# An S4 and quantized-FFN layer on one core: the first x parts paired, and gate/up block 0 cut into a chunk of its own

## The reference

```
x = x + 0.5 * ffn(layernorm(x));  x = x + s4(layernorm(x));  x = x + 0.5 * ffn(layernorm(x))

def _qlinear(x, q, scale, A, Bm):
    w = (q.astype(jnp.float32) - Q_ZERO) * (scale * Q_STEP)[:, None]
    y = jnp.einsum('bsh,oh->bso', x, w)
    return y + LR_SCALE * (x @ A @ Bm)

ffn(x) = _qlinear(silu(_qlinear(x, gate...)) * _qlinear(x, up...), down...)
s4(u)  = irfft(rfft(u, n=2L) * rfft(K, n=2L))[..., :L] + D * u      # K from the S4 state, L = 512
```

## Time and profile before

| what | value |
|---|---|
| median of three executions | 569.65 us (569.47 to 571.22) |
| the profiled execution | 569.99 us, span 568.2 us |
| PE busy | 556.5 us, 98% of the span |
| DVE, ACT, POOL busy | 427.2, 312.9, 256.4 us |
| PE clock granted over the span | full speed in every one of the 40 slices |
| bytes read from HBM, written | 15.90 MB, 4.19 MB |
| PE busy in 0 to 20 us, 20 to 64 us, 64 to 100 us | 20.00, 43.22, 35.26 us (pipelined matmuls overlap) |

### The profile page before, as it was taken

The page is one execution under the profiler, slowest core; times in us unless marked ns, Lnnn a source line. Parts: engine busy times, 40 slices in busy tenths (PEclk is TensorE's granted clock), DMA queues, the critical chain, the costliest instruction groups (busy, mean ns, idle before and its releaser), DMA issues.

```text
span 568.2 us, 12661 instructions
## 1 busy us (share of the span) xinstructions
PE 556.5 (98%) x4816; PEld 449.4 (79%) x4816; DVE 427.2 (75%) x824; ACT 312.9 (55%) x773; POOL 256.4 (45%) x272
## 2 busy tenths in 40 slices
PE   8999999989999999999999999999999999999997
PEld 8644678887688877888778887788877888788975
DVE  5789889996889957889578884598845987555544
ACT  5778425863168831688317883178731676246621
POOL 4379612664036850368503784037830477015510
PEclk9999999999999999999999999999999999999999
DMA  8985431009050190002900029000391104440002
GB/s 262 340 282 204 86 59 43 2 1 131 15 22 5 30 180 15 2 2 35 175 16 2 1 38 171 15 3 1 59 151 55 37 2 56 84 158 2 2 0 75
DMA packets 90804, 40.04 MB, mean 70 GB/s; under 512 B 79000, under 2 KB 84889, under 8 KB 90745
## 3 DMA queue, kind: packets, MB, share of 16 engines
q1 hardware_dynamic: 89849, 38.97, 31.3%
q10 hardware_dynamic: 896, 0.27, 0.2%
HBM read 15.90 MB, written 4.19 MB: 35 GB/s over the span
## 4 chain that ended last, share of the span: by engine, by line
PE 92%; DVE 5%; issue 1%; ACT 1%; DVEq 1%; POOL 0%; POOLq 0%; ACTq 0%
PE banks L1561 40%; PE banks L1480 28%; PE banks L1523 6%; PE banks L1537 5%; PE banks L1706 5%; PE banks L1432 2%; PE banks L1716 2%; PE banks L1500 1%; PE banks L1517 1%; PE banks L1726 1%; DVE X L1050 0%; DVE c_stats L1080 0%; DVE ring L1047 0%; DVEq L909 0%; PE banks L1415 0%
## 5 line engine op out<-in xcount | busy, mean ns | idle before, releaser
L1561 PE MATMUL banks<-xT,w 128*128 128x256 f16 (+1 forms) x2156 | 260.4, 273 | 1.5 <-DVE work L1006 1.4
L1561 PEld LDWEIGHTS banks<-xT,w 128*128 128x128 f16 (+1 forms) x2156 | 212.5, 100 | 26.3 <-DVE work L1006 2.7
L1480 PE MATMUL banks<-dw,hT 128*128 128x256 f16 (+3 forms) x1408 | 184.0, 286 | 0.0
L1480 PEld LDWEIGHTS banks<-dw,hT 128*128 128x128 f16 (+1 forms) x1408 | 135.4, 98 | 33.8 <-issue 0.4
L1006 DVE SCALAR_TENSOR_TENSOR work<-banks,work 128x512 f32<-128x512 f32 (+1 forms) x88 | 60.6, 688 | 43.4 <-PE banks L1523 27.4
L501 POOL TENSOR_TENSOR rstd<-veps,minus_half 128x1 f32<-128x1 f32 x32 | 19.6, 615 | 160.8 <-DVE veps L912 160.7
L571 POOL TENSOR_SCALAR hT<-work 128x512 f16<-128x512 f32 x70 | 44.2, 631 | 99.6 <-DVE work L1006 99.6
L574 POOL TENSOR_TENSOR hT<-work,hT 128x512 f16<-128x512 f32 x70 | 82.6, 1179 | 5.8
L1020 DVE SCALAR_TENSOR_TENSOR banks<-banks,scales,work 128x512 f32<-128x512 f32 (+1 forms) x77 | 57.7, 750 | 0.7 <-PE banks L1561 0.7
L1027 DVE SCALAR_TENSOR_TENSOR banks<-banks,scales,work 128x512 f32<-128x512 f32 (+1 forms) x77 | 57.7, 750 | 0.2 <-ACT work L807 0.2
L581 POOL TENSOR_TENSOR z<-zs,z 128x1024 f16<-128x1024 f32 (+1 forms) x28 | 55.5, 1992 | 4.5 <-ACT z L740 4.4
(11 more groups left out here) (191 smaller groups left out, 677.2 us busy)
## 6 DMA issues: line engine op xcount, KB each, us to landing
out_x<-X SPq DMA_DIRECT2D x15, 256.0 KB, 2.8
X<-in_x SPq DMA_DIRECT2D x1, 2048.0 KB, 9.9
ring<-in_gate_q_t SPq DMA_DIRECT2D x2, 768.0 KB, 9.5
hT<-in_up_q_t SPq DMA_DIRECT2D x2, 768.0 KB, 11.3
X<-in_b SPq DMA_DIRECT2D x2, 560.0 KB, 10.7
X<-in_x SPq DMA_DIRECT2D x1, 1024.0 KB, 14.3
ring<-in_down_q_t SPq DMA_DIRECT2D x1, 1024.0 KB, 12.5
X<-in_x SPq DMA_DIRECT2D x3, 256.0 KB, 5.0
```

The source lines that it names most:

```text
L1480: last = mm(acc(j)[:, 1 - c, 0:width], hT[0:rows[m], m, a, j * P:(j + 1) * P], dw[0:rows[m], m, src], start=(m == 0 and a == 0), stop=(m = ...
L1561: last = mm(dst[0:r, 0:HH], w[:, blocks + k, cols], xT[:, a, 2 * op + k, :], start=(first and k == 0 and a == 0), stop=(k == 1 and a == 1) ...
```

## The change

Three things are edited. The first two parts of x come in as one pair of transfers: SP loads both parts of partitions 0 to 63, ACT both parts of partitions 64 to 127, and DVE's statistics of part 0 and of part 1 both wait for the two transfers. `CHUNKS` becomes five groups: block 0 alone, then 1 to 3, 4 and 5, 6 and 7, and 8 to 10; the transfers of chunks 2 and 3 stand where chunk 2's stood. POOL casts chunk 0 ahead of the fourth rstd instead of behind it, chunk 3 right behind chunk 2, and chunk 4 where chunk 3 was cast; ACT casts chunks 2, 3 and 4 at m = 2, 4 and 6.

```diff
-CHUNKS = [(0, 2), (2, 5), (5, 8), (8, 11)]
+CHUNKS = [(0, 1), (1, 4), (4, 6), (6, 8), (8, 11)]
...
-            sp.dma_start(X[0:P // 2, 0, :], x_v[0:P // 2, 0, :]).then_inc(s_x[0], 16)
-            for j in range(1, TS):
+            sp.dma_start(X[0:P // 2, 0:2, :], x_v[0:P // 2, 0:2, :]).then_inc(s_x[0], 16)
+            for j in range(2, TS):
                 sp.dma_start(X[:, j, :], x_v[:, j, :]).then_inc(s_x[j], 16)
...
             chunk(2)
+            chunk(3)
             sp.dma_start(X[:, TS:2 * TS, :], x_v[:, TS:2 * TS, :]).then_inc(s_xrest[0], 16)
...
-            chunk(3)
+            chunk(4)
...
+            cast_gate(0)
             ln_rstd(0, 3)
-            cast_gate(0)
             cast_gate(1)
...
             cast_gate(2)
+            cast_gate(3)
             s4_real_parts()
             ln_rstd(1, 0, 1)
-            cast_gate(3)
+            cast_gate(4)
...
-            act.dma_start(X[P // 2:P, 0, :], x_v[P // 2:P, 0, :]).then_inc(s_x[0], 16)
+            act.dma_start(X[P // 2:P, 0:2, :], x_v[P // 2:P, 0:2, :]).then_inc(s_x[0], 16)
...
-                    if n == 0 and m in (2, 4):
+                    if n == 0 and m in (2, 4, 6):
                         cast_up(1 + m // 2)
...
-                dve.wait_ge(s_x[j], 32 if j == 0 else 16)
+                dve.wait_ge(s_x[j] if j > 1 else s_x[0], 16 if j > 1 else 32)
```

## The result

The changed kernel takes 572.45 us (median of 12 executions), the kernel before 569.88 us beside it (12). The ratio is 1.0036, with a 95% interval of 1.0024 to 1.0048: 2.1 us slower (1.4 to 2.7), outside the forecast range of 568.5 to 571.2. The profiled execution took 572.14 us, its span 570.5, against 569.99 and 568.2.

A forecast was written before the change was run, and what follows sets the result against it. PE was taken as the bound, busy 556.5 of 568.2 us. Start, loop and chain terms were each 0, so the forecast stayed at the median of the three runs, 569.7 us, range 568.5 to 571.2.

The forecast's parts named there:

- the term on `omega`: Landing of the omega tables on SP's queue, behind x and gate/up blocks: 0, bounds -0.3 and +0.4 us.
- The gain that was held against the descriptors: Start of the DMA stream: up to 0.7 us sooner if the quiet stretch shrinks, nothing won if it only moves.
- price per descriptor: Loads ahead of omega: 64 more descriptors per DMA engine at 6 ns fixed each, 0.4 us later.
- The pair's landing: Start: x's paired parts land at 4.5 us, 6.40 at the latest, costing only from 5.34 on; worth 0.
- rival B: Start: pair lands after 5.34 us, PE waits up to 0.85 us, end +0.3 to +0.85 us, 570.3; chance 0.13.
- It counts: Start: PE runs a fixed count of dummy matmuls to about 10.06 us without waiting for x; start term 0.
- The cast ahead of the fourth rstd: POOL's earlier cast near 11 us: could hold DVE up to 0.6 us, 0.25 reaching PE; part's sum 0.
- The casts in ACT's list: First tile's loop: 0.35 us won at blocks 4 to 6, lost at 7; +0.3 at block 8, absorbed later; net 0.
- The stand at 78.02 as a buffer: PE's 0.62 us stand: absorbs losses under 0.6 us ahead of it; PE's gains are waited away unless POOL is earlier.
- A: Omega and its chain come earlier by filling the quiet stretch: -0.3 to -0.6 us, 569.2; chance 0.14.
- C: POOL and DVE meet otherwise on the shared port: PE's 1.4 us wait goes, 568.3, or 1.7 us come, 571.4; chance 0.10.
- full clock throughout: Whole span: PE is busy 556.5 of 568.2 us at full clock, so only time in which PE stands can be won.

The follow-up runs named there:

- pair_only: Changed kernel with the old chunks and casts, so only x's first two parts are paired; 571.52 us, ratio 1.0031 to the kernel before.
- x_halves: Kernel before with part 1 of x also in two halves, on SP's and ACT's queues, waited for apart from part 0; 571.39 us, ratio 1.0020.
- late_start_b: Kernel before with 40 instead of 28 dummy matmuls between the transposes of parts 0 and 1, repeated with more rounds; 570.03 us, ratio 0.9996.
- before_again: Kernel before, run once more unchanged; 570.19 us (1 execution).
- after_again: Changed kernel, run once more unchanged; 572.85 us (1 execution).
- chunks_only: Changed kernel with the old x transfers, keeping the five chunks and their casts; 570.74 us, ratio 1.0024 to the kernel before.
- chunks_cast_m4: As chunks_only, with ACT's casts of chunks 3 and 4 both at m = 4, none at m = 6; 571.03 us, ratio 1.0010 to the kernel before.
- omega_mid: Kernel before with all three omega transfers moved ahead of the x of tile 1; 572.49 us, ratio 1.0030.
- warm_more: Kernel before with 106 instead of 96 dummy matmuls in the start; 569.91 us, ratio 0.9992.
- split_loads: Kernel before with each gate and up transfer of chunks 0 and 2 cut in two by columns, casts unmoved; 571.9 us, ratio 1.0028.
- after_omega_first: Changed kernel with all three omega transfers moved ahead of chunks 2 and 3; 573.72 us, ratio 1.0068 to the kernel before.

## Why the prediction was wrong

**The step that failed is the term on `omega`.** The prediction called it the one that "decides the end" and set it to 0, with bounds of -0.3 and +0.4. It measured +1.6 us (+1.9 in the first profile), and DVE's z, PE's stands and the end followed. Why SP's queue brings the tables later isn't settled: the runs show where it falls behind, not what holds it. The term was wrong in three ways.

*The gain that was held against the descriptors did not exist.* The -0.3 came from filling the quiet stretch at 3.0 to 4.4 us. The stretch moved behind the pair, as the text had allowed; what it had not allowed is that the stream is later for it. It took "nothing is won" as the bad case, while the full rate began a microsecond later, and `pair_only` has the tables 0.7 to 0.8 us late. The bound on that side was one of gains alone.

*Transfers were priced by their bytes and descriptors.* `x_halves` moves the same bytes of x in the same row sizes, with one transfer more, on ACT's queue, and has its tables 2 us late in its one profile. A price per descriptor, from two stretches at full rate, doesn't hold what the split itself costs.

*No bound looked at SP.* Its issues in the changed kernel fall behind at chunks 2 and 3, now four transfers: the first of them goes out at 13.31 (12.23 before), the x of tile 1 behind them at 19.70 (14.92), the third table at 22.84 (20.33); the second profiles of both kernels have 13.27 and 12.53, 19.74 and 15.44, 22.88 and 20.86. SP's queue was treated as a list of bytes ahead of `omega`, but single issues on it took 0.4 to 3.1 us ahead of the third table. Its rows were in the trace of before.

**The pair's landing**, taken as 4.5 us, was 5.60 (5.53 and 5.49 in the two later profiles). That is behind the 5.34 from which rival B priced it. B's mechanism came true only in small: the low half of part 0 ended at 9.90 instead of 9.64. PE's wait of 0.66 us for it came for the most part from dummy matmuls that ended earlier, at their faster rate from 5.8 us on instead of 7.4 (last section); the first transposes are 0.07 us later than before, the second, at 12.41, 0.51. B's low price of +0.3 for a late start of 0.85 fits what `late_start_b` shows (0.77 us late, 0.29 at the end), but the changed kernel's time is beyond B's 570.3 by way of the tables.

**"It counts"** was half true. In the start PE's dummy matmuls ended without a wait in the first profile of before, but in `before_again` PE already waited 0.17 us for z, at 9.99. The count's end moves with the moment at which PE's rate changes, so it leaves no room that a reader could rely on.

**The cast ahead of the fourth rstd** held DVE for 0.35 us in the first profile and 0.19 in the second, within the up to 0.6 that had been feared. This is POOL's, then DVE's row in the changed kernel:

```profile
11.20 0.62 POOL L509 TENSOR_SCALAR w<-ring 128x512 f16<-128x512 int32 x1 [0.25 <-DMA hT<-in_up_q_t]
```

```profile
11.32 1.03 DVE L927 TENSOR_TENSOR z<-zs,z 128x512 f16<-128x512 f32 x1
```

The same instruction took 0.68 us before, so 0.35 us came from the cast; with part 2's statistics 0.24 us later (8.15 against 7.91) they make PE's 0.52 us. The Trainium skill's "SBUF — State Buffer", section "Who interferes with whom", has DVE wait to the end of POOL's instruction. By that DVE would have ended near 12.50 (11.82 and its own 0.68); it ended at 12.35, so the two rows fit the rule to 0.15 us. The prediction had 0.25 us of it come through to PE; PE was 0.51 late at 12.41, 0.26 in `after_again`.

**The casts in ACT's list** did what was said, in size smaller. PE's stand at block 4 went from 0.30 to 0.17 us (low-rank matmul at 33.59, product at 33.98, less 0.22), not to nothing, since h of block 2 was late from DVE; in `chunks_only`, where it wasn't, the whole 0.30 went, as forecast. The new cast ran from 49.01 to 50.37, and z could be rounded at 50.28, 0.2 us later than the 2.1 us delay alone explains. One wait was overlooked: DVE's sum of the up weights needs the last up cast, which is now at m = 6.

```profile
50.41 0.88 DVE L1280 TENSOR_TENSOR w<-w 128x1376 f16<-128x1376 f16 x1 [0.37 <-ACT w L870]
```

It held DVE for 0.37 us. `chunks_cast_m4` doesn't have this wait, and its time isn't told from that of `chunks_only`.

**The stand at 78.02 as a buffer** was a second wrong step, though not the one that decided. The prediction let it absorb any loss under 0.6 us ahead of it, the 0.3 us of the new cast among them. It is 0.61 or 0.62 us in every profile, and what PE has lost by 61 us is still lost behind it: 0.33 and 0.29 in `late_start_b`, 0.71 and 0.72 in `pair_only`, 2.30 and 2.17 in the changed kernel. The 0.13 that comes back in the last is at the low-rank matmul at 64 us, and no more than 0.18 came back there in any profile. What took up PE's lateness in `late_start_b` were the stands at blocks 4, 7 and 8.

**The other rivals.** A, tables earlier, had the wrong sign twice: they came later, and where they were made earlier (`omega_mid`) the kernel lost too. C did not happen; the 1.4 us wait is still 1.4.

## What to carry to other kernels

Where a late table ends in the last stand that counts, read that table's landing as the sum of all that its queue does from the first transfer on, and give the start of the queue a bound on the loss side as wide as the stretch it could move: here a quiet stretch of 1.4 us, taken as a chance to win, became 0.8 us lost. Splitting early transfers for finer arrival, or laying them on a second engine's queue, is not free for what stands 19 transfers behind. Before moving such a table ahead, see what lands later for it and what then runs side by side: here a cast that began 1.4 us later met DVE's small instructions and cost the loop more than the wait had. And before a stand is counted as a buffer, see in a second profile whether it shrinks when what is ahead of it comes late: this one never did.

## What the runs showed of the hardware

**A larger first transfer starts later.** With 64 partitions x 2 rows of 2 KB on each of two queues the engines moved 63 GB/s from 2 to 3 us (78 to 139 in the other four profiles with the pair), with one row each 262 (248 to 277 in the other ten that can be read).

**A clock of 1.00 in the start isn't a reading.** The trace's record of the granted clock begins at 7.37 us in the first profile of before and at 5.77 in the changed kernel's; for the time ahead of it the views print 1.00. The starts of single dummy matmuls in the traces show what PE did: 107 ns apart until 7.38 and 5.78 us, 56 ns from there on, close to the ratio of the clock's two levels (1.2 and 2.4 GHz). In all 16 profiles the pace changes within 0.06 us of where the record begins, at 4.7 to 7.6 us. So the stretches above ran at the lower level up to that moment, and "full clock throughout" in the prediction doesn't hold for them. What sets the moment isn't shown. It is why ten more dummies in `warm_more` took no longer: their pace changed at 6.20 us, 1.2 us sooner.

**Small DVE instructions wait out a POOL cast.** A DVE instruction of two columns took 1.45 us instead of 0.22 in `omega_mid` and 1.47 instead of 0.45 in `split_loads`, each begun 0.03 to 0.06 us behind a cast of POOL and ended within 0.03 us of it. The 0.45 us is that of the kernel before, where the instruction began 1.04 us behind the cast and ended with it too. So what is left of the cast is the price, and a load that lands a microsecond later can raise it by a microsecond.

**A drop of the clock behind one wait splits the executions in two.** Of 98 executions of the kernel before, 69 had a mean granted clock of 0.998 or more and a median of 569.67 us, and 29 had less, and 571.32. Where it is seen it lies at one place, shown by `after_again` (first fence) and `before_again` (second), with PE alone listed, then the granted clock, the DMA share and the GB/s:

```profile
155.00:160.00 5.00, 3.17 (x25) 0.92 0.00 0
160.00:165.00 5.00, 5.00 (x36) 0.74 0.50 28
165.00:170.00 5.00, 5.00 (x48) 1.00 0.79 28
```

```profile
155.00:160.00 5.00, 3.17 (x28) 1.00 0.06 13
160.00:165.00 5.00, 5.00 (x48) 1.00 0.58 19
```

In both PE had stood 1.56 us for `pd_stack` and then 0.27 us. In the one the clock then fell to the lower of its two levels (1.2 instead of 2.4 GHz), by the trace's record for 3.41 us from 159.22 on, and 46 matmuls took 6.69 us instead of 5.18; in the other it did not. Half the pace for 3.41 us costs 1.7 us, which is the 1.65 between the two medians. `x_halves`, `after_omega_first` and `chunks_cast_m4` have the same drop, at 158.3 to 160.9 us. It is the larger part of the scatter of the kernel before: among the executions at 0.998 or more, the changed kernel has 571.68 us (7), and 569.67 is before's, a difference of 2.0 us.
